# Decoder layer on one core: half of the keys' projection of the first step placed ahead of the probability transposes

## The reference

```python
def reference(x, ctx, mask, ...):
    x = x + attn(layernorm(x))        # one head of 512, blocks of 128 rows, causal, softmax
    x = x + xattn(layernorm(x), ctx)  # 16 heads of 32, 64 keys per batch, silu instead of softmax
    x = x + ffn(layernorm(x))         # 512 -> 2048 -> 512, gelu

# in xattn, for the context ctx (4 x 64 x 512) as key and value:
    k = split_heads(ctx @ Wk.T + bk)
    v = split_heads(ctx @ Wv.T + bv)
```

## Time and profile before

| what | us |
|---|---|
| median of 3 runs | 1269.24 (1269.16 to 1270.24) |
| profiled execution | 1269.33 |
| its span, first to last instruction | 1266.9 |
| PE busy in it | 1250.7 |
| DVE, ACT, POOL busy | 665.5, 487.4, 244.3 |

### The profile page before, as it was taken

One profiled execution on the slowest core, in us unless ns is written; L12 is line 12 of the kernel. 1 busy time (PEld: TensorE's weight loads), 2 busy tenths in 40 slices (PEclk: granted clock), 3 DMA queues, 4 the chain that ended last, 5 costly groups with the idle time before them and its releaser, 6 DMA issues.

```text
span 1266.9 us, 15607 instructions
## 1 busy us (share of the span) xinstructions
PE 1250.7 (99%) x5785; PEld 1039.4 (82%) x5785; DVE 665.5 (53%) x1210; ACT 487.4 (38%) x887; POOL 244.3 (19%) x225
## 2 busy tenths in 40 slices
PE   9989999999999999999999999999999999999998
PEld 7878888888888888867888888888888888888887
DVE  7476858585858585856733443333424334433211
ACT  7246555545454545444332222322222322223221
POOL 2303232323232313138601002001001010020000
PEclk9999999999999999999999999999999999999999
DMA  8210202020202020316210010010100100100000
GB/s 294 81 63 13 76 14 75 13 75 12 75 12 75 12 75 12 125 40 210 75 67 1 1 67 1 1 66 0 36 30 0 66 0 0 66 0 0 34 1 34
DMA packets 40486, 60.04 MB, mean 47 GB/s; under 512 B 4224, under 2 KB 14464, under 8 KB 40448
## 3 DMA queue, kind: packets, MB, share of 16 engines
q1 hardware_dynamic: 40448, 59.53, 14.1%
HBM read 41.17 MB, written 18.35 MB: 47 GB/s over the span
## 4 chain that ended last, share of the span: by engine, by line
PE 54%; DMA 1%; SPq 0%; DVE 0%; ACT 0%; issue 0%; DVEq 0%
PE bank L50 18%; PE bank L52 18%; PE bank L51 18%; DMA w_raw<-in_w 0%; DMA x_dram<-resid 0%; DVE resid L1166 0%; SPq L1049 0%; DVE w_parts L185 0%; ACT w_parts L181 0%; SPq L1047 0%; SPq L189 0%; SPq L1046 0%; DVEq L1165 0%; SPq L1056 0%
## 5 line engine op out<-in xcount | busy, mean ns | idle before, releaser
L1156 DVE TENSOR_TENSOR hid_lo<-gelu_out,hid_hi 128x512 fp32r<-128x512 f32 x128 | 98.2, 767 | 399.1 <-ACT gelu_out L1123 399.0
L50 PE MATMUL bank<-zT,w_parts 128*128 128x512 f32 x768 | 299.3, 390 | 4.9 <-DVE zT L150 1.8
L52 PE MATMUL bank<-zT,w_parts 128*128 128x512 f32 x768 | 298.8, 389 | 0.0
L51 PE MATMUL bank<-zT,w_parts 128*128 128x512 f32 x768 | 298.8, 389 | 0.0
L1119 ACT ACTIVATE hid_hi<-bank,b_col 128x512 fp32r<-128x512 f32 x128 | 88.3, 690 | 491.0 <-PE bank L52 491.0
L50 PE MATMUL bank<-w2p_hi,hid_lo 128*128 128x512 f32 x512 | 199.3, 389 | 0.7 <-DVE hid_lo L1156 0.7
L52 PE MATMUL bank<-w2p_hi,hid_hi 128*128 128x512 f32 x512 | 199.2, 389 | 0.0
L51 PE MATMUL bank<-w2p_lo,hid_hi 128*128 128x512 f32 x512 | 199.2, 389 | 0.0
L50 PEld LDWEIGHTS bank<-zT,w_parts 128*128 128x128 f32 x768 | 144.2, 188 | 36.7 <-issue 3.0
L51 PEld LDWEIGHTS bank<-zT,w_parts 128*128 128x128 f32 x768 | 144.2, 188 | 29.8
L52 PEld LDWEIGHTS bank<-zT,w_parts 128*128 128x128 f32 x768 | 144.0, 188 | 29.9
(11 more groups left out here) (141 smaller groups left out, 1811.0 us busy)
## 6 DMA issues: line engine op xcount, KB each, us to landing
x_in<-in_x SPq DMA_DIRECT2D x32, 256.0 KB, 3.7
x_dram<-resid SPq DMA_DIRECT2D x32, 256.0 KB, 2.1
w_raw<-in_w SPq DMA_DIRECT2D x32, 256.0 KB, 3.4
resid<-x_dram SPq DMA_DIRECT2D x32, 256.0 KB, 3.1
out_dram<-resid SPq DMA_DIRECT2D x32, 256.0 KB, 2.1
resid<-in_wqkvT SPq DMA_DIRECT2D x12, 256.0 KB, 4.8
mask_i<-in_mask SPq DMA_DIRECT2D x16, 128.0 KB, 2.6
values_now<-values_dram SPq DMA_DIRECT2D x8, 256.0 KB, 2.8
```

Of the source, the lines that this page charges most:

```text
L50: pe.matmul(out_ap, lhs[1], rhs[0], start=start, stop=False)
L51: pe.matmul(out_ap, lhs[0], rhs[1], start=False, stop=False)
L52: return pe.matmul(out_ap, lhs[0], rhs[0], start=False, stop=stop)
L1156: dve.tensor_tensor(hid[1][:, c % 4, :], gelu_out[:, c % 2, :], f(hid[0][:, c % 4, :]), ALU.subtract).then_inc(hid_lo, 1)
```

## The change

The keys' bank pair goes from (3, 4) to (5, 3): chunks 0 and 1 are written to bank 5, chunks 2 and 3 to bank 3. A helper computes a list of chunks and raises `keys_done` at its end. In the first step chunks 0 and 1 are computed behind value rows 3 and ahead of the wait for `prob_ready`, and chunks 2 and 3 where all four stood. ACT, DVE, POOL and SP keep their order.

```diff
-KEY_BANK = (3, 4)
+KEY_BANK = (5, 3)
...
+                        def keys(chunks_):
+                            for m in chunks_:
+                                for c in range(EC):
+                                    last = product(pe, key_chunk(m), at(wk, c, cols(m)),
+                                                   at(ctx2, c, slice(None), 0), c == 0, c == EC - 1)
+                            last.then_inc(keys_done, 1)
+
...
                             else:
                                 value_rows(2)
                                 value_rows(3)
+                                keys((0, 1))
                             pe.wait_ge(prob_ready, NB * (a + 1))
...
                             else:
-                                for m in range(EC):
-                                    for c in range(EC):
-                                        last = product(pe, key_chunk(m), at(wk, c, cols(m)),
-                                                       at(ctx2, c, slice(None), 0), c == 0, c == EC - 1)
-                                    if m % 2 == 1:
-                                        last.then_inc(keys_done, 1)
+                                keys((2, 3))
```

## The result

The changed kernel takes 1272.61 us (median of 10 runs, 1271.85 to 1274.41), the kernel before 1269.65 us (median of 10, 1269.1 to 1270.8): 2.96 us more, a ratio of 1.0023 with a 95% interval of 1.0015 to 1.0031. The forecast was 1272.2 us, 1270.4 to 1273.6. The profiled execution is one of the two slowest of the ten, 1274.41 us with a span of 1271.9, so its own account is 5.0 us over the earlier trace rows.

The account below looks back on a forecast made before the run. PE is busy 1250.7 of 1266.9 us, so its waits in the first step and the start of the second decide. Terms 0 + 1.43 + 1.5 = +2.93 us gave 1272.2 us, range 1270.4 to 1273.6.

Parts of the forecast that it names:

- (a): At the probability transposes: 24 keys' matmuls ahead of them push them by the whole 2.88 us, no wait there.
- (b): Wait for the probabilities' low part, behind their transposes: 0.18 us gained (bounds 0 and 1.57), product 2.70 later.
- (c): Behind the probability product: residual, norm and row transposes 2.70 us later, PE idle some 3.0 us instead of 0.19.
- (d): Other queues: key store and ACT's key blocks stay in place, loads of x slip 2.7 us, all hidden.
- (e): Second step's chunk scores: their 1.00 us wait vanishes, so the 2.70 us shift shrinks to +1.43.
- (f): Query projection: the 3.0 us stand ahead makes the clock fall to 1.2 GHz, costing 1.5 us (0 to 2.5).
- Rival 1: Clock holds through the 3.0 us stand, leaving only +1.43 us: 1270.7 us; chance 0.37.
- Rival 2: Wait at the chunk scores stays, nothing absorbed: +2.70, 1271.9 us with a held clock (chance 0.05), 1273.4 with a fall.
- Rival 3: Moved matmuls fill the 1.57 us wait ahead of the probability product, not slower at all: 1267.7 us; chance 0.05.

Follow-up runs that it names:

- early transposes: Kernel before, with the probability transposes moved ahead of value rows 3 and the probabilities taken ahead of value chunk 3: 1268.28 us against 1269.90, ratio 0.9987.
- filled kernel: Changed kernel plus 12 matmuls of 512 columns behind keys 2 and 3, result unread: 1271.69 us, ratio 1.0014 to the kernel before.
- half the push: Changed kernel with 12 of the keys' matmuls in front instead of 24, 36 behind the product: 1269.35 us, ratio 1.0001 to the kernel before.
- 12 in the other gap: Changed kernel with 12 keys' matmuls between probability transposes and the low-part wait, 36 behind the product: 1269.62 us, ratio 0.9998 to the kernel before.
- the split store alone: Kernel before, with SP storing and loading back batch 0 of the keys ahead of storing the other three: 1269.90 us, ratio 0.9998.
- pushed and covered: Changed kernel with keys 0 and 1 computed twice, in front and again behind the product with all four chunks: 1272.15 us against 1269.90 before.

## Why the prediction was right

**(a) and (b), the push.** 24 matmuls took 71.20 - 68.33 = 2.87 us, as reckoned, and the wait behind the transposes lost 0.16 where 0.18 was said. The product came 2.70 later with the offset of the start taken off: exactly the term.

**(c), the cover.** The stand ahead of the row transposes was 3.08 us, forecast 3.0. Filling it took nothing back of the push, and giving PE its cover back by more keys didn't either: the row transposes come 2.71 and 2.70 us later than before. PE's busy share is no help in reading this place: the step goes by the chain from the probability product over DVE and POOL to the normed rows, and only what makes that product earlier is won. The early transposes show it from the other side: product 1.01 earlier, queries 0.85.

**(d) and (e), what is absorbed.** The store and the key blocks kept their places (80.01 and 86.51), and the wait of 1.00 us was gone. The filled kernel gives 1.56 at the scores for the worked-out 1.54, and 1.67 us in time for 1.43; with the store slipping along, 2.61 at the scores and +2.25 in time for 2.70. The mechanism is shown by the profiles of the two.

**(f), the clock.** The fall was the forecast's riskiest step. It is there in the profiled execution, one of the two slowest; the other eight were 1271.85 to 1272.79 us and have no profile. All ten runs have a mean clock of 0.999 or less, against four of eleven with the stand filled. Its price was put at 1.5 us, with a bound of 2.5 for the queries and 0.8 for the transposes. The profiled execution paid 2.00 us in the queries and 1.23 in their later start (87.27 + 0.18 - 86.22), so 3.2. For the median, what is left when the push of the filled kernel is taken off is 2.96 - 1.67 = 1.3; this is a remainder, and no run measured it by itself.

**Where it was lucky.** The forecast of +2.93 for the measured +2.96 is closer than its terms: the push came out 0.24 above its term in time and the rest 0.2 below. The upper bound of the low stretch, 5.1 us from the kernel's start, was wrong: it lasted 10.2 us. The 2.5 us for the queries held only because these began 6.0 us after the fall, and the late transposes cost 1.23 where 0.8 was left for them. At the start the level was taken from the pace of the matmuls, every 0.45 us; the profile's granted clock reads 1.00 there. In the low stretches here the pace is 0.43. And the forecast's own range comes out of its terms as 1271.7 to 1274.0 (2 us low cost 1.0; 2.5 and 0.8 together 3.3), not 1271.4 to 1273.8.

**What was wrong in it.** Two sentences of (f) didn't hold. The step reasoned that a stand longer than 2.6 us brings the fall and that the kernel before, with 0.19 and 1.84, keeps its clock. The changed kernel's clock had already fallen 2.2 us after PE's last matmul. The clock fell with stands of 1.64 and 1.83 us (half the push, 12 in the other gap), and with the split store alone, whose stands of 0.20 and 1.83 are those of before. Behind the last matmul of the program, where the 2.6 was read, three other profiles have the fall 2.5, 2.8 and 3.2 us later, and six have none in the 3.3 us to their end. So 2.6 us was one instance and no limit.

How often the clock falls at the queries isn't known, as a run's mean clock counts any low stretch, at its very end too. It is below 1.000 in all ten runs of the changed kernel and in 4 of 11 with the stand filled, which differ in the 12 matmuls only (and in the session): that the long stand makes it likelier is shown. For short stands it is not: below 1.000 are 5 of 11 with half the push, 7 of 11 with 12 in the other gap, 1 of 11 pushed and covered, and 36 of 66 of the kernel before. There such runs are hardly slower (1269.74 against 1269.74 on one chip, 1270.09 against 1269.86 on the other). That fits the wait of 1.00 us at the scores: a fall of 3.4 us costs 1.6 in the queries, and in the two profiles with the queries unmoved only 0.45 of it arrives at the scores.

**Rival 1**, a clock that holds, is what the filled kernel makes: 1271.7 us, not the 1270.7 given, and every run of the changed kernel was above both. **Rival 2**, nothing absorbed, is what the covered kernel shows once the store slips. **Rival 3**, the filled wait as a gain, fails on the place: the wait lies behind the transposes. Even the 12 matmuls set in the very gap moved the idle time to the next wait, and the queries began where they did.

The Trainium skill, "TensorE: Matmul & The Clock Gate", section "What's actually happening", has activity release the throttle; the filled kernel agrees with it in this case, as with 12 matmuls whose result nobody reads the granted clock was 1.00 from 81 to 90 us, where it had been 0.50 to 0.55.

## What to carry to other kernels

Work that stands behind a product on PE may be the cover of another engine's chain. Before moving it, look at what PE would wait for next: if that wait is nearly zero (here 0.19 us) the cover is exact, and what is moved ahead is paid behind it (2.70 us for 24 matmuls, 1.26 for 12), until a later wait takes some of it. A wait is filled by what stands between its cause and itself, not by what stands ahead of the cause, and filling it wins time only if something downstream moves earlier.

A few microseconds of thin work and waits on PE can halve the clock for the dense work that follows: here one fall cost 1.6 us in three profiles and 3.2 in a fourth. In such a place look at the runs' spread and the granted clock of windows, not at one profile. And before two profiles are compared by their times, line them up at a matmul that both have ahead of the edit.

## What was not expected of the hardware

The fall doesn't wait for a stand: with half the push it came when the queries had run for some 1.5 us at full rate, behind thin transposes and a stand of 1.83 us. One and the same program gave 1268.91 to 1269.51 or 1271.72 to 1272.36 us, and the profile with the fall is of the slower group. With the split store it came 0.7 us after the queries had begun, with no stand above 1.83 us ahead. The low stretch was 3.4 us long in three profiles and 10.2 in the changed kernel's. And row transposes at the low level took 3.67 us for sixteen, not 2.02: the norm ahead of them was on time, but ACT and DVE behind them had to wait for each block.
